# A graph layer's first stage: loads in another order, edge tables spread by products, other places for the roots

## The reference, cut to what matters

```python
xn = _layernorm(x)                      # x: 3125 x 256
h = einsum('ni,hio->hno', xn, W)        # 4 heads of 64
attn_src = einsum('hno,hod->hn', h, a_src)
attn_dst = einsum('hno,hod->hn', h, a_dst)
e = attn_src[:, src] + attn_dst[:, dst] # 50000 edges, sorted by dst
e = where(e >= 0, e, 0.2 * e) * edge_weight
e_exp = exp(e - max(e))
denom = segment_sum(e_exp, dst)
out = segment_sum(h[:, src] * e_exp / (denom[dst] + 1e-10), dst)
x = x + out + linear_attention(xn, W_qkv, W_out, b_out)
x = x + ffn_on_the_top_half_of_the_tokens(_layernorm(x), wr, w1, w2)
```

## Time and profile before

| | us |
|---|---|
| median of 3 runs | 785.09 |
| lowest and highest | 783.83 and 785.42 |
| profiled execution | 783.45 |
| its span, first to last instruction | 781.6 |
| busy: TensorE, VectorE, GpSimd, ScalarE | 622.1, 534.2, 452.8, 182.9 |

### The profile page before, as it was taken

One profiled execution on the slowest core, in us unless ns is written; L12 is line 12 of the kernel. 1 busy time (PEld: TensorE's weight loads), 2 busy tenths in 40 slices (PEclk: granted clock), 3 DMA queues, 4 the chain that ended last, 5 costly groups with the idle time before them and its releaser, 6 DMA issues.

```text
span 781.6 us, 12836 instructions
## 1 busy us (share of the span) xinstructions
PE 622.1 (80%) x3279; PEld 509.8 (65%) x3280; DVE 534.2 (68%) x1295; ACT 182.9 (23%) x651; POOL 452.8 (58%) x511
## 2 busy tenths in 40 slices
PE   2786676777777777889878978887759999999995
PEld 2653455655566656667656665665648899999994
DVE  8724665666566656566757766676769982999994
ACT  2542110112121211111211211212224433333231
POOL 4217677777677777667777777677701350434314
PEclk9997888888878887797978987977779999999998
DMA  8268455554455555444544555455400002010100
GB/s 228 80 129 251 112 133 131 137 135 135 124 134 135 135 130 131 114 127 132 131 125 128 142 133 129 111 138 132 111 8 1 1 1 85 28 35 28 34 15 30
DMA packets 61659, 81.61 MB, mean 104 GB/s; under 512 B 30893, under 2 KB 42299, under 8 KB 61469
## 3 DMA queue, kind: packets, MB, share of 16 engines
q0 software_dynamic: 18816, 52.21, 24.8%
q1 hardware_dynamic: 41597, 27.41, 13.7%
q10 hardware_dynamic: 1184, 1.18, 0.5%
HBM read 74.11 MB, written 6.64 MB: 103 GB/s over the span
## 4 chain that ended last, share of the span: by engine, by line
POOL 26%; DVE 26%; issue 19%; PE 18%; DMA 5%; DVEq 2%; ACT 2%; SPq 1%; ACTq 0%; POOLq 0%
POOL G L398 25%; DVE xnT L1182 6%; DVE xnT L1185 5%; PE ps L506 5%; DMA G<-htab,srcr 3%; PE ps L636 3%; PE ps L623 2%; PE ps L441 2%; PE ps L584 2%; DVE msg L966 2%; DVE stats L821 1%; DVE G L1127 1%; PE ps L454 1%; DVE x L1131 1%; DVEq L246 1%
## 5 line engine op out<-in xcount | busy, mean ns | idle before, releaser
L398 POOL DMA_INDIRECT G<-htab,srcr x392 | 374.3, 955 | 145.1 <-issue 133.3
L506 PE MATMUL ps<-msg,oh 128*128 128x260 f32 x784 | 225.2, 451 | 23.0 <-DVE msg L966 17.5
L506 PEld LDWEIGHTS ps<-msg,oh 128*128 128x128 f32 x784 | 178.3, 232 | 62.3 <-issue 27.1
L966 DVE TENSOR_TENSOR msg<-G,ps 128x1024 f32<-128x1024 f32 x98 | 115.3, 1218 | 25.8 <-ACT ps L742 25.1
L741 ACT ACTIVATE msg<-et,negR 128x32 f32<-128x32 f32 x49 | 15.8, 322 | 364.2 <-DVE rj L961 363.6
L623 PEld LDWEIGHTS ps<-xnT,w 128*128 128x128 f32 x800 | 95.3, 196 | 3.9 <-issue 1.8
L623 PE MATMUL ps<-xnT,w 128*128 128x128 f32 x800 | 95.8, 279 | 2.1 <-ACT wide L802 1.6
L636 PE MATMUL ps<-w,wide 128*128 128x256 f32 x400 | 90.7, 380 | 2.5 <-DVE acc L1151 2.5
L636 PEld LDWEIGHTS ps<-w,wide 128*128 128x128 f32 x400 | 74.1, 190 | 12.3 <-issue 3.3
L416 POOL TENSOR_SCALAR G<-acc,mw 128x256 f32<-128x256 f32 x23 | 21.2, 923 | 94.4 <-DVE mw L1190 34.7
L482 PE MATMUL ps<-ad,ohT 128*128 x584 | 44.5, 207 | 25.8 <-DVE ohT L935 13.5
(11 more groups left out here) (154 smaller groups left out, 703.5 us busy)
## 6 DMA issues: line engine op xcount, KB each, us to landing
dstb<-dstu_d SPq DMA_DIRECT2D x49, 256.0 KB
G<-htab,srcr POOLq DMA_INDIRECT x392
htab<-hst SPq DMA_DIRECT2D x25, 130.0 KB, 2.4
out<-G SPq DMA_DIRECT2D x24, 128.0 KB, 1.7
w<-in_L_ffn_w SPq DMA_DIRECT2D x4, 512.0 KB
kT<-w_d SPq DMA_DIRECT2D x1, 1600.0 KB, 6.4
x<-in_x SPq DMA_DIRECT2D x2, 640.0 KB, 9.5
srcr<-in_src SPq DMA_DIRECT2D x48, 4.0 KB
```

Source lines behind the costliest of these rows:

```text
L398: gp.indirect_dma_start(G[:, q % RING, k, :], None, htab, bass.IndirectOffsetOnAxis(ap=srcr[:, q, k:k + 1], axis=0)).then_inc(s_g[q % RING ...
L506: m = pe.matmul(sums_of(p), oh[:, p, k, :], msg[:, k, :], start=(k == 0), stop=(k == TILES - 1))
L966: dve.tensor_tensor(msg[:, tiles, 0:HF].rearrange("p k (h o) -> p k h o", h=HEADS), G[:, q % RING, tiles, 0:HF].rearrange("p k (h o) -> p ...
```

## The change

- GpSimd: the addition that made iotab, and the iota that it read, go; five iotas of 640 columns stand among the clearings instead. It makes the 16-bit cast that ScalarE made. Its gathers wait for the source list alone, which has a semaphore of its own.
- VectorE: the identity needs five constants instead of fourteen; the PSUM copy and the comparison stand at block 10. The weights' product with the attention vectors stands ahead of the statistics of blocks 1 to 4, which come in two pairs with a root each. The ten table steps stand at blocks 8, 9, 13 and 14.
- Loads: SP takes one half of the weights and blocks 1 to 4, ScalarE the other half and blocks 5 to 9. The attention vectors go to one partition and are spread by a product with a row of ones into PSUM.
- Ranges and low targets: copied to floats at block 15, brought to one partition and to all by four products with the identity on TensorE at block 17, taken from PSUM by VectorE at block 19. Their four DMAs go.
- ScalarE: the roots stand in other places of its order.
- TensorE: twelve products with the identity stand ahead of the first projection; the third key chunk stands between the two expansions.
- SP: edge lists of the first four groups are loaded during the stage instead of behind it.

```diff
 @@ constants and places
+        SRC_AT, LISTS_AT, CASTS_AT, DST_AT = 2, 8, 12, 17
+        RANGES_AT = 17
+        WARM_AT_START = 12
 @@ SP
                 sp.dma_start(x[:, 0:1, :], x_in[0:P, :].rearrange("(b p) c -> p b c", p=P)).then_inc(s_x[0], 16)
-                for kc in range(KC):
-                    sp.dma_start(wbig[:, kc, 0:HF].rearrange("k (h o) -> k h o", h=HEADS),
...
+                load_weights(sp, 0)
                 for which, array in enumerate((gas_in, gad_in)):
-                    sp.dma_start(avec[:, which, :], array.rearrange("(a h) o b -> a (h o b)", a=1).to_broadcast([P, HF])).then_inc(S["a_loaded"], 16)
+                    sp.dma_start(avec[:, which, :], array.rearrange("(a h) o b -> a (h o b)", a=1)).then_inc(S["a_loaded"], 16)
+                base, blocks = NORMED[1]
+                sp.dma_start(x[:, base:base + blocks, :], ...
...
                 for t in range(NB):
                     store_rows(t)
-                    if t == TABLES_AT:
-                        store_tables()
-                    if t == TABLES_AT + 6:
-                        spread_tables()
-                    if t in LISTS_AT:
-                        step(LISTS_AT.index(t), LISTS_AT.index(t))
-                unrolled(step, range(len(LISTS_AT), LISTS))
+                    if SRC_AT <= t < SRC_AT + LISTS:
+                        columns_of(t - SRC_AT, t - SRC_AT, False, ((srcr, src_in),))
+                    if LISTS_AT <= t < LISTS_AT + LISTS:
+                        columns_of(t - LISTS_AT, t - LISTS_AT, False, ((wtr, ew_in), (dcr, dst_in)))
...
+                    if t == CASTS_AT:
+                        store_casts()
+                    if t == DST_AT:
+                        sp.wait_ge(S["tables_stored"], 16)
+                    if DST_AT <= t < DST_AT + LISTS:
+                        destinations(t - DST_AT, t - DST_AT)
 @@ GpSimd
-            gp.wait_ge(S["constants_ready"], 14)
-            gp.tensor_tensor(iotab, iota[:, :].unsqueeze(1).to_broadcast([P, NB, P]), blkbase[:, :].unsqueeze(2).to_broadcast([P, NB, P]), ALU.add).then_inc(S["block_iota_ready"], 1)
             for t in range(NB):
                 gp.wait_ge(S["xn_ready"], t + 1)
                 gp.memset(acc[:, t, :], 0.0).then_inc(S["acc_zeroed"], 1)
+                if t == 2 * BODY - 2:
+                    gp.wait_ge(S["dst_loaded"], 48)
+                    gp.tensor_copy(du[:, :], dl[:, :]).then_inc(S["table_cast"], 1)
+                if t % BODY == BODY - 1:
+                    lo = (t + 1 - BODY) * P
+                    gp.iota(wide[:, lo:lo + BODY * P], [[1, BODY * P]], base=lo, channel_multiplier=0, allow_small_or_imprecise_dtypes=True).then_inc(S["block_iota_ready"], 1)
...
-                gp.wait_ge(s_list[q], lists)
+                gp.wait_ge(s_src[q], lists)
 @@ TensorE
+            pe.wait_ge(S["a_loaded"], 32)
+            pe.matmul(ps[:, 4, 0:2 * HF], ones[:, :], avec[:, :, :].rearrange("a s n -> a (s n)"), start=True, stop=True).then_inc(S["a_spread"], 1)
             for t in range(NB):
+                if t == 1:
+                    for _ in range(WARM_AT_START):
+                        pe.matmul(ps[:, 5, 0:P], ident[:, :], ident[:, :], start=True, stop=True)
+                    project(0)
...
-                if t:
+                if t >= 2:
                     project(t - 1)
+                if t == RANGES_AT:
+                    pe.wait_ge(S["table_floats"], 2)
+                    for c in range(3):
+                        pe.matmul(ps[0:1, 4, c * NG:(c + 1) * NG], mf[:, c:c + 1], ident[0:NG, 0:NG], start=True, stop=True)
+                    pe.matmul(ps[:, 4, 3 * NG:4 * NG], mf[:, 3:4].to_broadcast([NG, P]), ident[0:NG, 0:NG], start=True, stop=True).then_inc(S["ranges_turned"], 1)
...
             expand(0)
+            keys(2)
             expand(1)
-            for c in range(2, CHUNKS):
+            for c in range(3, CHUNKS):
 @@ ScalarE
                 if t == 1:
-                    deviation(1, BODY - 1, BODY)
-                if t == 2:
+                    deviation(1, 2, 3)
+                if t == BODY - 1:
                     deviation(BODY, BODY, 2 * BODY)
-                if t == 3:
-                    act.wait_ge(S["dst_loaded"], 48)
-                    act.activation(du[:, :], dl[:, :], ACT.Copy).then_inc(S["table_cast"], 1)
-                if t % BODY == 4 and t + BODY + 1 < NB:
-                    deviation(t + 1 + BODY, BODY, t + 1 + 2 * BODY)
+                if t % BODY == 0 and t and t + BODY < NB:
+                    deviation(t + BODY, BODY, t + 2 * BODY)
                 act.wait_ge(S["xn_turned"], t + 1)
                 act.activation(xnT[:, t, :, :], ...
+                if t == 1:
+                    deviation(3, BODY - 3, BODY)
 @@ VectorE
+            dve.wait_ge(S["a_spread"], 1)
             dve.wait_ge(S["w_loaded"], 32)
...
+            dve.wait_ge(s_x[1], 16)
+            statistics(1, 2, 1)
+            invert(1, 2, 2)
...
             for t in range(NB):
                 i, j = t // BODY, t % BODY
+                if i in (1, 2) and j >= 3:
+                    edge_tables(2 * (i - 1) + j - 3)
+                if t == RANGES_AT - 2:
+                    dve.wait_ge(S["table_steps"], DLP)
+                    dve.tensor_copy(mf[:, 0:3], mm[:, :]).then_inc(S["table_floats"], 1)
+                    dve.tensor_copy(mf[:, 3:4], dn[:, 6:7]).then_inc(S["table_floats"], 1)
+                if t == RANGES_AT + 2:
+                    dve.wait_ge(S["ranges_turned"], 1)
+                    dve.tensor_copy(meta[:, 0:NG * 3].rearrange("a (g c) -> a c g", c=3), ...).then_inc(S["ranges_ready"], 1)
...
                 if i + 2 < NB // BODY:
-                    for k in ((0, 1), (2,), (3,), (4,), ())[j]:
+                    for k in ((0, 1), (2, 3), (4,), (), ())[j]:
                         one_block_statistics((i + 2) * BODY + k)
-                    if j == BODY - 1:
-                        invert((i + 2) * BODY, BODY, i + 4)
+                if j == 0 and i and i + 1 < NB // BODY:
+                    invert((i + 1) * BODY, BODY, i + 4)
...
+            take_keys(0)
+            take_keys(1)
             dve.wait_ge(S["attn_dst_last"], 1)
             columns(1)
```

More of the change, by code:

```diff
@@ L200, in gps_layer @@
         s_list = [sem(f"s_list{i}") for i in range(LISTS)]
+        s_src = [sem(f"s_src{i}") for i in range(LISTS)]
         s_g = [sem(f"gathered{i}") for i in range(RING)]
@@ L849, in _ @@
             m.then_inc(S["w_a_ready"], 1)
[L850 to L851 removed]
+            dve.wait_ge(s_x[1], 16)
+            statistics(1, 2, 1)
+            invert(1, 2, 2)
+            for t in range(1, 3):
+                normed(t).then_inc(S["xn_ready"], 1)
+            dve.wait_ge(S["mean_var_ready"], 3)
+            statistics(3, BODY - 3, 3)
+            invert(3, BODY - 3, 3)
+            for t in range(3, BODY):
                 normed(t).then_inc(S["xn_ready"], 1)
```

152 lines of the change are left out of this document (78 added, 74 removed).

## The result

The kernel after takes 772.08 us (median of four runs, 771.32 to 773.01) against 784.46 (781.00 to 785.42, four runs) for the kernel before: a ratio of 0.9851, 95% interval 0.9823 to 0.9880. Its profiled execution took 771.74 us with a span of 769.9; the one of before took 783.45 with 781.6.

What follows compares the result with a forecast made beforehand. GpSimd's stream of 392 gathers bounds the kernel. The stage ends 8.1 + 1.6 + 2.1 - 2.0 = 9.8 us earlier, plus 2.9 at the 17th gather: 12.7 off the 785.09 median gives 772.4, range 767.5 to 778.

Steps and rivals of the forecast that it cites:

- Start: Head of the first stage: weights at 9.2, block 5 normalised at 17.8, projection 4 at 18.3, 8.1 us earlier.
- Warming products: Twelve TensorE products ahead of the first projection: 3.2 to 6.4 us, covered by VectorE's calendar; uncovered, up to 2.6 lost.
- Clock: TensorE's clock taken as up in the projections, regaining 1.6 us from block 4 to block 9.
- The wait at block 17: TensorE waits at block 17 for VectorE's float copies, 1.5 us, plus 0.5 for four small products: 2.0 lost.
- rival (3): VectorE is ahead at block 17 and the wait costs only 0.5 us: 770.1 us; chance 0.08.
- The slot stall: ScalarE's 2.97 us wait for a store to free its staging slot goes: 2.1 us gained on TensorE.
- The stall: GpSimd's 3.21 us idle ahead of the 17th gather: that gather gains 2.9 us over the stage, bounds 1.5 and 2.9.
- clock as before: Key chunks: moving one chunk ahead saves the rest of the chain 1.5 us if the clock stays low.
- (1): GpSimd's iotas and cast lock VectorE in the stage, 3.7 us going into block 17's wait: 776.1 us; chance 0.18.
- (2): Clock stays low in the warming products and the keys, 2.6 and 1.4 us lost: 776.4 us; chance 0.08.
- (4): The gather stream does not follow the stage's end, so nothing moves: 785 us; chance 0.03.
- (5): VectorE's pacing pauses hold TensorE at the lower clock in the whole stage: 799.1 us; chance 0.03.

Runs made afterwards that it cites:

- three kernels with x on time: Kernel after, first stage unchanged: third key chunk moved back (770.63 us), late weight loads held (772.22), or held with six identity products (770.79).
- split_x: Kernel after with x of blocks 1 to 4 cut into two loads, on SyncE's and ScalarE's queues: 772.21 us.
- no_warm: Kernel after without the twelve warming products at the start: 772.75 us.
- roots_later: Kernel after with ScalarE's roots for blocks 10 on moved one evacuation later: 771.63 us.
- tiny_stores: Kernel after with two unread DRAM stores of 49 tiny rows added behind the cast table's store: 778.18 us.
- gpsimd_doubled: Kernel after with GpSimd's cast and each of its five iotas issued twice: 771.95 us.
- iotas_only: Kernel before with only GpSimd's 5.62 us addition exchanged for five iotas: 783.68 us, ratio 1.0004.
- addition_back: Kernel after with GpSimd's 5.62 us addition back in place of the five iotas: 773.97 us.
- the six products: Six identity products on TensorE where it waits for VectorE's comparison, added to the kernel after with late weight loads held: 770.79 us.

## Why the prediction held, point by point

The forecast was 772.4, the median is 772.08. The mechanism is the one that was named: the first stage ends earlier, the stall ahead of the 17th gather goes, and the stream follows at its old pace. The steps behind it were less exact than the sum, and that the sum came within 0.3 us is in part luck: misses of up to 1.6 us cancel, and the landing of x alone moves the end of the stage by more than 1 us from trace to trace.

- *Start.* Block 0 at 4.52 (4.6 predicted) and the weights at 8.73 (9.2) came as worked out. "I take no delay" for blocks 1 to 4 was wrong in the profiled run: they landed 1.14 us late, inside the bound of 1.5. In the other runs VectorE waited between nothing and 0.6, so this term is a spread and not a value. Block 5 was normalised at 18.60 (17.8) and projection 4 started at 18.93 (18.3): 7.45 instead of 8.1 gained. In the three kernels with x on time it started at 17.60 to 17.88, 8.5 to 8.8 earlier than before.
- *Warming products.* 4.99 us, between my 3.2 and 6.4, and covered here by the late x; in split_x (5.33) they were not. What no_warm shows is that they buy some 0.6 us.
- *Clock.* Up, as predicted: 1.06 to 1.16 a projection in the whole stage. From block 4 to block 9 it is 6.66 us, before 7.29; the 1.6 are regained, and the next point takes 1.0 of them.
- *ScalarE's root at block 5.* Missing from my sum. I moved the roots and didn't ask which copy stands behind them; it cost 1.0, and roots_later gets it back.
- *The wait at block 17.* Mis-sized: 0.8 instead of 2.0. VectorE's calendar was too long: the 16.6 us that I had added up took 14.9 (18.60 to 33.49), since in the timeline an instruction starts before the one ahead of it ends (18.20 for 0.40, the next at 18.52). And TensorE came 1.3 us later than worked out, at 34.3, so that it waited for nothing. That is rival (3), in part.
- *The slot stall.* Gone, and for the reason given: tiny_stores brings it back with two tiny stores.
- *Stage end.* 43.94 for 43.7: the late x and the root (1.6 together) and the wait at block 17 (1.2 the other way) nearly cancel.
- *First gather.* 49.11 for 48.2. I had carried the 4.48 us from the last projection over; it was 5.17. The runs show 3.7 to 5.4 and do not say what sets it.
- *The stall.* 0.30 is left of 3.21 and the 17th gather comes 20.24 behind the first (20.2 predicted). The size of this term was right in the profiled run and its cause was not: I gave it to the order of the chunks. The runs show it with the clock, and in three kernels of the same order 1.3 to 1.6 of the 2.9 are given back. My bound of 1.5 for "clock as before" was about what those runs have. The 0.6 that was to stay of the stall at the late end does not go with that bound: I had the 17th gather released 1.2 behind the start of the message product, and it starts 2.01 behind it, before as in every kernel whose product comes late.
- *Sum.* 12.7 predicted, 11.76 at the 17th gather and 12.4 between the medians. Of the range, the lower end (767.5) lies 2.6 under rival (3) with no term given for it.

Of the rivals, (1) has its mechanism confirmed and its price refuted by gpsimd_doubled. (2) is half there: by their pace (24 in 4.99 us) the warming products ran near the lower level, but covered, and the keys did in some runs, for some 1.5 us each. (4) and (5) did not happen: the stream followed the stage in every kernel, and the clock stayed at 1.00 from 25 to 40 us. Of the parts, in the presence of the others, by the first gather against the kernel after and against the three with x on time: the tiny stores are worth 4.3 or 5.6 to 6.1 us, the places of the roots 2.3 or 3.5 to 4.0, the addition 2.0 or 3.3 to 3.8. The warming products are worth some 0.6 ahead of projection 4, the order of the keys nothing that can be told. These don't add up to the whole, since each hides behind the next, as iotas_only and addition_back show for one of them. The order of the loads with the spread attention vectors, the places of VectorE's table steps, and the early loads of the edge lists were not taken out by themselves: that the first two bring projection 4 forward is read from the timelines alone.

## What to carry to other kernels

Find the event at which a long stream is released and follow every edit to that event in the timeline: here fourteen profiles differ by 13.5 us and all but some 2 us to either side is in the start of one instruction. When an instruction is moved ahead of others on its engine, list what is queued behind it for the case that its own input is late, and take the same list for its old place. A cost that hides behind another is worth nothing by itself and its full size after the other is gone, so take parts out of the new kernel as well as adding them to the old one. And hold a trace against several with the same code ahead of the event: one landing that came late in the trace of the kernel after makes the tiny stores and the places of the roots look 1 to 2 us cheaper than traces with the same landing on time do.

## What the runs showed of the hardware that was not expected

- Two stores of 49 tiny rows each (0.6 and 0.2 KB in all) on SyncE's queue kept five row stores of 130 KB behind them from freeing a slot for 5.09 us (landing 7.1 to 8.5 us after issue); without them the same five cost no wait (2.4 to 3.0).
- The granted clock in the same key chunks, in kernels that are alike from there on, was 1.00 or at times 0.50 over 4 us, which are its two levels of 2.4 and 1.2 GHz; the chunks took 7.7 to 10.8 us. A pause of TensorE of 1.2 us lies ahead of them in all kernels without the six products, so the pause alone does not say which it will be.
- GpSimd's addition of two SBUF tables held a VectorE normalisation until 0.15 us behind its end (4.00 for 0.41), but the statistics beside it ran at 0.43. An iota of 0.66, which reads no table, held one as well (0.87 for 0.40), and so did a clearing of 0.32 (0.60).
- In no_warm the clock column reads 1.00 from 8 to 14 us, where projections take 2.10 and 2.13 instead of 1.06. There the durations are the row to read.
